# Moving one multiply per tile from VectorE to GpSimd, and column sums behind the next group's matmuls, in an eight-core layer kernel

## The chip, the cores and the metric

The kernel runs on the 8 NeuronCores of one Trainium2 chip, one batch element to a core, with no exchange between cores. The metric is the device time in microseconds of the slowest core. The profile is that of the slowest core (core 1).

## The reference

One layer over x of 8 x 2048 x 2048. A complex diagonal recurrence, a layer norm, a gated feed-forward block with weights rounded to -1, 0, 1 and activations rounded to 8 bits, and a second layer norm. The part that matters here is the second projection:

```python
def _act_quant(a):
    scale = QB / clip(max(abs(a), axis=-1), 1e-05)
    return clip(round(a * scale), -QB, QB) / scale
def _weight_quant(w):
    s = clip(mean(abs(w)), 1e-05)
    return clip(round(w / s), -1.0, 1.0) * s
h = value * silu(gate)                                  # (T, 8192)
h = einsum('bsd,od->bso', _act_quant(h), _weight_quant(w_out))
x = _layernorm(x + (x + h))
```

## The kernel before

Each core works on transposed tensors: features on the partitions, the 2048 time steps along the free dimension. Three stages come before the one of interest: the recurrence, the first layer norm and quantisation, and the gated projection of 64 pairs, which writes h2 (8192 x 2048, bf16) to `h2sp` and the rounded output weights to `wq2sp`. They fill the time up to about 3850 us and are not touched.

The last stage makes the output projection for four blocks q of 512 time steps. `d_mm(q, seg)` does half of the contraction (32 tiles of 128 of h2) for all 2048 outputs, in eight groups dg of two output tiles (ds 0 and 1) each. A group loads its weights in four blocks of 512 KB from the GpSimd queue (L975), into the two halves of `WR`, and runs 16 matmuls on each block (L986). The results of a group go to PSUM banks 0 and 1 of psA, 2 and 3 of psA, or 0 and 1 of psB, in turn. In seg 0 they are copied to `P2` by ScalarE (L1001). In seg 1 there is an epilogue for each of the two tiles: a load of the residual x1 (L1012, on ScalarE's queue), PSUM plus P2 on VectorE (L1018), a product with the scale on GpSimd (L1023), twice x1 added on VectorE (L1028), a store to `z2sp` (L1035), the column sum of the tile by a matmul with ones (L1040), the square on ScalarE (L1048), and the column sum of the squares (L1053). The two sums pile up in banks 3 and 2 of psB.

The moving operand P1 is made by `d_chain(q, seg, j)`, once for each of the 64 tiles of a block: a load of h2 on SyncE's queue (L942) into one of 8 slots of `CBF`, a multiply by the scale (L948) into one of two f32 buffers (`CH_HS` for even j, a part of `MNA` for odd j), and `round_neg`, five steps on VectorE (L246, L248, L250, L253, L256), the last of which writes P1. The 32 chains of (0, 0) are emitted ahead of all groups (`d_quant`); all others are fed between groups: `d_mm` takes a list of functions, and after each group runs the share of it that is due, `take = ceil(rest / groups left)`. While q's seg 0 runs, the chains of its seg 1 are fed, and then the `tail` of the block before: `d_rowsL` (row statistics, two broadcasts through TensorE) and 16 `d_apply_a` (the final norm of one tile each: a load, two GpSimd products L1091 and L1096, a store L1101). While seg 1 runs, the chains of the next block's seg 0 are fed. `d_rowsQ(q + 1)` makes the scale rows of the next block, with two broadcasts that use banks 2 and 3 of psB.

Every engine runs its instructions in the order in which the code emits them. The order is that of the calls; the class `B` adds the waits. It keeps the last writer and the readers of each region, a region being 2 KB of a partition (`GR`), so that two neighbouring 1 KB slots of `CBF` are one region. A wait stands in an engine's queue ahead of the instruction that needs it, and holds all that comes after it.

Of the kernel before, what the change touches and what calls it, by code (L numbers as in the profile page):

```python
# [19 lines left out]
NQ = 4  # L20
# [8 lines left out]
def R(name, e0, e1, es=4):  # L29
    b0, b1 = e0 * es, e1 * es  # L30
    return [(name, i) for i in range(b0 // GR, -(-b1 // GR))]
# [74 lines left out]
def build_program(debug=False):  # L106
    nc = bass.Bass("TRN2", target_bir_lowering=False)
    b = B()
# [828 lines left out]
    def d_chain(q, seg, j):  # L937
        par = q % 2
        jo = seg * 32 + j
        hq = jo % 8  # L940
        hsl = j % 2
        b.dma("sync", lambda s, q=q, jo=jo, hq=hq: s.dma_start(  # L942
            out=CBF[:, hq * 512:(hq + 1) * 512],
            in_=h2sp_t[:, jo, q * 512:(q + 1) * 512]),
            reads=[("h2sp", jo, q // 2)],
            writes=R("CBF", hq * 512, (hq + 1) * 512, es=2))
        src_ap, src_regs = RN[hsl][0], RN[hsl][1]
        b.op("vector", lambda v, hq=hq, src_ap=src_ap, par=par: v.tensor_tensor(  # L948
            src_ap, CBF[:, hq * 512:(hq + 1) * 512], S2B[par],
            OP.mult),  # L950
            reads=R("CBF", hq * 512, (hq + 1) * 512, es=2) +
                  S2R[par],
            writes=src_regs)
        round_neg(hsl,
                  P1[:, seg * 16384 + j * 512:seg * 16384 + (j + 1) * 512],
                  R("P1", seg * 16384 + j * 512,
                    seg * 16384 + (j + 1) * 512, es=2))
# [5 lines left out]
    def d_mm(q, seg, feeder=()):  # L963
        feeder = list(feeder)
        fi = 0
        par = q % 2
        for dg in range(8):
            d0 = dg * 2
            rot = dg % 3
            PSm = [lambda k: PSA(k), lambda k: PSA(2 + k), lambda k: PSB(k)][rot]  # L970
            RRm = [lambda k: RA(k), lambda k: RA(2 + k), lambda k: RB(k)][rot]
            for blk in range(4):
                gj = seg * 32 + blk * 8
                sl = blk % 2
                b.dma("gpsimd", lambda g, dg=dg, gj=gj, sl=sl: g.dma_start(  # L975
                    out=WR[:, sl * 2048:(sl + 1) * 2048].rearrange(
                        "p (j c) -> p j c", j=8),
                    in_=wq2sp[dg, gj // 8]),
                    reads=[("wq2sp", j) for j in range(gj, gj + 8)],
                    writes=R("WR", sl * 2048, (sl + 1) * 2048, es=2),  # L980
                    q="Dwq")
                for jj in range(8):
                    jl = blk * 8 + jj
                    for ds in range(2):
                        b.op("tensor", lambda t, jl=jl, jj=jj, ds=ds, sl=sl,
                             seg=seg, PSm=PSm: t.matmul(  # L986
                            PSm(ds),
                            WR[:, sl * 2048 + jj * 256 + ds * 128:
                               sl * 2048 + jj * 256 + (ds + 1) * 128],
                            P1[:, seg * 16384 + jl * 512:  # L990
                               seg * 16384 + (jl + 1) * 512],
                            start=(jl == 0), stop=(jl == 31)),
                            reads=R("WR", sl * 2048, (sl + 1) * 2048, es=2) +
                                  R("P1", seg * 16384 + jl * 512,
                                    seg * 16384 + (jl + 1) * 512, es=2),
                            writes=[RRm(ds)] if jl in (0, 31) else [],
                            inc=((jj == 7 and ds == 1) or jl == 31))
            if seg == 0:
                for ds in range(2):
                    t_ = dg * 2 + ds  # L1000
                    b.op("scalar", lambda s, ds=ds, t_=t_, PSm=PSm: s.copy(  # L1001
                        P2[:, t_ * 512:(t_ + 1) * 512], PSm(ds)),
                        reads=[RRm(ds)], writes=R("P2", t_ * 512, (t_ + 1) * 512))
                take = -(-(len(feeder) - fi) // (8 - dg))
                for _ in range(take):
                    feeder[fi]()
                    fi += 1
                continue
            for ds in range(2):
                a = d0 + ds  # L1010
                t_ = dg * 2 + ds
                b.dma("scalar", lambda s, q=q, a=a, ds=ds: s.dma_start(  # L1012
                    out=X1S[:, ds * 512:(ds + 1) * 512],
                    in_=x1sp_t[:, a:a + 1, q * 512:(q + 1) * 512]),
                    reads=[("x1sp", a, q)],
                    writes=R("CBF2", ds * 1024, (ds + 1) * 1024, es=2),
                    q="Dscalar")
                b.op("vector", lambda v, ds=ds, t_=t_, PSm=PSm: v.tensor_tensor(  # L1018
                    Z2S[:, ds * 512:(ds + 1) * 512], PSm(ds),
                    P2[:, t_ * 512:(t_ + 1) * 512], OP.add),  # L1020
                    reads=[RRm(ds)] + R("P2", t_ * 512, (t_ + 1) * 512),
                    writes=R("Z2S", ds * 512, (ds + 1) * 512))
                b.op("gpsimd", lambda g, ds=ds, par=par: g.tensor_tensor(  # L1023
                    Z2S[:, ds * 512:(ds + 1) * 512],
                    Z2S[:, ds * 512:(ds + 1) * 512], DQB[par], OP.mult),
                    reads=R("Z2S", ds * 512, (ds + 1) * 512) + DQR[par],
                    writes=R("Z2S", ds * 512, (ds + 1) * 512))
                b.op("vector", lambda v, ds=ds: v.scalar_tensor_tensor(  # L1028
                    Z2S[:, (2 + ds) * 512:(3 + ds) * 512],
                    X1S[:, ds * 512:(ds + 1) * 512], 2.0,  # L1030
                    Z2S[:, ds * 512:(ds + 1) * 512], OP.mult, OP.add),
                    reads=R("CBF2", ds * 1024, (ds + 1) * 1024, es=2) +
                          R("Z2S", ds * 512, (ds + 1) * 512),
                    writes=R("Z2S", (2 + ds) * 512, (3 + ds) * 512))
                b.dma("scalar", lambda s, q=q, a=a, ds=ds: s.dma_start(  # L1035
                    out=z2sp_t[:, a:a + 1, q * 512:(q + 1) * 512],
                    in_=Z2S.ap().rearrange("p (s t) -> p s t", s=4)[:, 2 + ds, :]),
                    reads=R("Z2S", (2 + ds) * 512, (3 + ds) * 512),
                    writes=[("z2sp", a, q)], q="Dscalar")
                b.op("tensor", lambda t, ds=ds, dg=dg: t.matmul(  # L1040
                    psB[0:1, 1536:2048], c_onesc[:],
                    Z2S[:, (2 + ds) * 512:(3 + ds) * 512],
                    start=(dg == 0 and ds == 0), stop=(dg == 7 and ds == 1)),
                    reads=R("Z2S", (2 + ds) * 512, (3 + ds) * 512) + [("c_onesc", 0)],
                    writes=[RB(3)] if (dg, ds) in ((0, 0), (7, 1)) else [],
                    inc=True)
                sqo = 2048 + ds * 512
                b.op("scalar", lambda s, ds=ds, sqo=sqo: s.activation(  # L1048
                    P3[:, sqo:sqo + 512], Z2S[:, (2 + ds) * 512:(3 + ds) * 512],
                    AF.Square),  # L1050
                    reads=R("Z2S", (2 + ds) * 512, (3 + ds) * 512),
                    writes=R("P3", sqo, sqo + 512))
                b.op("tensor", lambda t, ds=ds, dg=dg, sqo=sqo: t.matmul(  # L1053
                    psB[0:1, 1024:1536], c_onesc[:], P3[:, sqo:sqo + 512],
                    start=(dg == 0 and ds == 0), stop=(dg == 7 and ds == 1)),
                    reads=R("P3", sqo, sqo + 512) + [("c_onesc", 0)],
                    writes=[RB(2)] if (dg, ds) in ((0, 0), (7, 1)) else [],
                    inc=True)
            take = -(-(len(feeder) - fi) // (8 - dg))
            for _ in range(take):  # L1060
                feeder[fi]()
                fi += 1

    def d_rowsL(q):
        b.op("vector", lambda v: v.tensor_scalar(
# [42 lines left out]
    tail = []  # L1108
    for q in range(NQ):
        f0 = [(lambda q=q, j=j: d_chain(q, 1, j)) for j in range(32)] + tail  # L1110
        d_mm(q, 0, f0)
        if debug and q == 0:
            b.dma("sync", lambda s: s.dma_start(out=tapA2[:], in_=P1[:]),
                  reads=R("P1", 0, DT * T, es=2), q="Dout")
        if q + 1 < NQ:
            d_rowsQ(q + 1)
            f1 = [(lambda q=q, j=j: d_chain(q + 1, 0, j)) for j in range(32)]
        else:
            f1 = []
# [89 lines left out]
```

How the kernel before makes its waits and increments, by code:

```python
            def emit(engobj, ename):  # L1136
                for item in b.stream[ename]:
                    if item[0] == "w":
                        engobj.wait_ge(semh[item[1]], item[2])
                    else:
                        instr = item[1](engobj)
                        if item[2] is not None:
                            instr.then_inc(semh[item[2]], item[3])
```

## Time and profile before

| | us |
|---|---|
| median of 2 runs | 5914.73 (5914.22 to 5915.24) |
| profiled execution, its own time | 5934.24 |
| span of its slowest core | 5932.6 |
| spans of the eight cores | 5894.7 to 5932.6 |
| granted TensorE clock of the cores | 0.806 to 0.811 |
| busy over the span: TensorE, VectorE, ScalarE, GpSimd | 58%, 43%, 24%, 11% |

The busy shares are means over stages that differ; the section after the next one holds rows of the last stage. Times in the rows are microseconds, counted from the start of the span. In a timeline row they are the start and the duration, then the engine, the line of the code, the operation, what it writes and reads, and in brackets how long the engine was idle before it and what ended that. DVE is VectorE, ACT ScalarE, POOL GpSimd, PE TensorE.

### The profile page before, as it was taken

The page shows a single profiled execution, that of the slowest core. Times are in us where ns is not written, and L with a number is a line of the kernel's source. Part 1 is how long each engine was busy: PE and PEld are TensorE (multiplying, and loading weights), DVE is VectorE, ACT ScalarE, POOL GpSimd, SP SyncE. Part 2 cuts the span into 40 slices and gives each one's busy share as a digit, 9 for nine tenths or more (in the row PEclk, how much of TensorE's full clock was granted, in tenths as well). Part 3 has the DMA queues.
Part 4 walks back from the last instruction along what each step waited for, and adds up shares of the span by engine and source line. Part 5 has one row for each costly group of instructions (what it writes and reads, how often), then busy time and mean ns, then how long its engine had stood idle before and what let it go on. Part 6 is the DMA issues. An engine that isn't in the chain of part 4 may idle for free.

```text
span 5932.6 us, 43701 instructions; the slowest of 8 cores (5894.7 to 5932.6 us)
## 1 busy us (share of the span) xinstructions
PE 3460.7 (58%) x13489; PEld 1332.3 (22%) x13489; DVE 2559.3 (43%) x3497; ACT 1404.4 (24%) x1134; POOL 645.8 (11%) x805
## 2 busy tenths in 40 slices
PE   1223321404888787777767799737782674476273
PEld 0100000001333333332323244302231221122121
DVE  1331844845333333333333344487673466158101
ACT  2222122132554444433444433200000000000000
POOL 0210000000000000000000000001112211311314
PEclk9866765756999898888888899859896887788686
DMA  8223445364555455565556632114442442343233
GB/s 220 78 92 106 130 155 168 127 213 159 184 192 186 159 140 146 135 136 130 145 131 143 131 101 94 39 57 129 134 147 77 127 138 93 114 129 123 97 114 105
DMA packets 211694, 774.78 MB, mean 131 GB/s; under 512 B 24412, under 2 KB 61439, under 8 KB 161799
## 3 DMA queue, kind: packets, MB, share of 16 engines
q10 hardware_dynamic: 64512, 318.80, 16.4%
q0 software_dynamic: 68832, 243.32, 14.9%
q1 hardware_dynamic: 78120, 209.87, 12.7%
q8 instruction: 110, 1.80, 0.1%
q14 instruction: 120, 0.98, 0.1%
HBM read 662.83 MB, written 117.44 MB: 132 GB/s over the span
## 4 chain that ended last, share of the span: by engine, by line
DMA 35%; PE 21%; DVE 17%; ACT 11%; issue 10%; POOL 5%; DVEq 1%; ACTq 0%; POOLq 0%; SPq 0%
DMA WOF<-woutT 8%; PE psA L986 6%; DMA WOF<-wgvL 5%; DMA WR<-wgvL 5%; DMA wq2sp<-P 4%; PE psA L784 4%; PE psB L784 4%; DMA WR<-wq2sp 3%; ACT HBF L734 3%; DMA WR<-woutT 3%; DMA CBF<-x1sp 2%; ACT P L745 2%; ACT WR L748 2%; DVE HBF L796 2%; ACT CBF L730 2%
## 5 line engine op out<-in xcount | busy, mean ns | idle before, releaser
L986 PE MATMUL psA<-P,WR 128*128 128x512 bf16 x3072 | 730.9, 396 | 414.4 <-DMA WR<-wq2sp 309.7
L784 PE MATMUL psA<-P,CBF 128*128 128x512 bf16 x2048 | 510.6, 410 | 233.5 <-DVE CBF L738 223.9
L784 PE MATMUL psA<-P,MNA 128*128 128x512 bf16 x2048 | 506.6, 407 | 211.6 <-DVE MNA L738 202.1
L986 PEld LDWEIGHTS psA<-P,WR 128*128 128x128 bf16 x3072 | 300.2, 101 | 878.2 <-issue 575.0
L784 PE MATMUL psB<-P,CBF 128*128 128x512 bf16 x2048 | 457.4, 379 | 9.6
L784 PE MATMUL psB<-P,MNA 128*128 128x512 bf16 x2048 | 457.4, 379 | 9.6
L752 DVE TENSOR_TENSOR P<-P,WR 128x2048 bf16<-128x2048 bf16 x64 | 78.4, 1226 | 739.2 <-ACT WR L748 739.2
L784 PEld LDWEIGHTS psA<-P,CBF 128*128 128x128 bf16 x2048 | 210.8, 104 | 532.0 <-issue 341.4
L784 PEld LDWEIGHTS psA<-P,MNA 128*128 128x128 bf16 x2048 | 209.8, 103 | 506.9 <-issue 313.4
L398 ACT ACTIVATE WOF<-WOF 128x2048 f32<-128x2048 f32 x96 | 183.5, 1911 | 402.8 <-DMA WOF<-wgvL 258.3
L745 ACT ACTIVATE P<-WOF,colS 128x2048 bf16<-128x2048 f32 x64 | 128.2, 2003 | 615.8 <-DMA wq2sp<-P 335.5
L1048 ACT ACTIVATE P<-Z2S 128x512 f32<-128x512 f32 x64 | 40.4, 631 | 978.4 <-DVE Z2S L1018 519.6
L398 ACT ACTIVATE WR<-WR 128x2048 f32<-128x2048 f32 x96 | 183.5, 1911 | 359.9 <-DMA WR<-wgvL 247.1
L806 ACT ACTIVATE HBF<-HBF 128x1024 f32<-128x1024 f32 x128 | 135.2, 1056 | 515.1 <-DVE HBF L796 515.1
L784 PEld LDWEIGHTS psB<-P,CBF 128*128 128x128 bf16 x2048 | 197.8, 98 | 264.1 <-issue 39.3
L784 PEld LDWEIGHTS psB<-P,MNA 128*128 128x128 bf16 x2048 | 197.7, 98 | 264.2 <-issue 39.3
L734 ACT ACTIVATE HBF<-P,colS 128x2048 bf16<-128x2048 f32 x128 | 254.4, 1988 | 0.0
L809 DVE TENSOR_TENSOR CBF<-CBF,HBF 128x1024 bf16<-128x1024 f32 x128 | 156.9, 1225 | 223.8 <-ACT HBF L806 223.8
L975 POOL DMA_DIRECT2D WR<-wq2sp x256 | 137.4, 537 | 1045.6 <-PE psA L986 780.5
L986 PE MATMUL psB<-P,WR 128*128 128x512 bf16 x1024 | 232.6, 384 | 30.3 <-DMA WR<-wq2sp 30.3
L834 POOL DMA_DIRECT2D h2sp<-CBF x128 | 70.4, 550 | 1545.3 <-DVE CBF L809 1369.8
L225 PE MATMUL psA<-REP,c_ones 1*128 1x512 f32 x16 | 15.4, 1059 | 348.6 <-DVE REP L582 204.2
(217 smaller groups left out, 4169.3 us busy)
## 6 DMA issues: line engine op xcount, KB each, us to landing
P<-wgvL SPq DMA_DIRECT2D x128, 1024.0 KB
WR<-wq2sp POOLq DMA_DIRECT2D x256, 512.0 KB, 3.9
WOF<-woutT ACTq DMA_DIRECT2D x96, 1024.0 KB, 6.6
WOF<-wgvL ACTq DMA_DIRECT2D x64, 1024.0 KB, 5.0
WR<-wgvL ACTq DMA_DIRECT2D x64, 1024.0 KB, 5.0
h2sp<-CBF POOLq DMA_DIRECT2D x128, 256.0 KB, 4.5
WR<-woutT ACTq DMA_DIRECT2D x32, 1024.0 KB, 5.1
wq2sp<-P POOLq DMA_DIRECT2D x64, 512.0 KB, 8.4
```

Source lines behind the costliest of these rows:

```text
L398: b.op("scalar", lambda s, slot=slot, buf=buf: s.activation(buf, buf, AF.Abs, accum_out=slots[:, slot:slot + 1]), reads=breg, writes=breg ...
L730: b.op("scalar", lambda s, sl=sl: s.activation(WQap(sl), WV[:, sl * 2048:(sl + 1) * 2048], AF.Sign, bias=colS[:, 1:2]), reads=R("P2", sl * ...
L734: b.op("scalar", lambda s, sl=sl, SGa=SGa: s.activation(SGa, WV[:, sl * 2048:(sl + 1) * 2048], AF.Sign, bias=colS[:, 0:1]), reads=R("P2", ...
L745: b.op("scalar", lambda s: s.activation(WOQ[:, 0:2048], WOF[:], AF.Sign, bias=colS2[:, 1:2]), reads=R("WOF", 0, 2048) + [("colS2", 0)], wr ...
L748: b.op("scalar", lambda s: s.activation(WR[:, 2048:4096], WOF[:], AF.Sign, bias=colS2[:, 0:1]), reads=R("WOF", 0, 2048) + [("colS2", 0)], ...
L752: b.op("vector", lambda v: v.tensor_tensor(WOQ[:, 0:2048], WOQ[:, 0:2048], WR[:, 2048:4096], OP.add), reads=R("P3", 2048, 3072) + R("WR", ...
L784: sv=sv, last=last: t.matmul(PS[:, (vg * 2 + tq) * 512:(vg * 2 + tq + 1) * 512], WQap(sv + vg)[:, a * 128:(a + 1) * 128], P1[:, a * T + th ...
L796: b.op("vector", lambda v, PS=PS, th=th: v.tensor_tensor(GS[:, 0:1024], PS[:, 1024:2048], dqa1rep[:, th * 1024:(th + 1) * 1024], OP.mult), ...
L806: b.op("scalar", lambda s: s.activation(SIL[:, 0:1024], GS[:, 0:1024], AF.Silu), reads=R("HBF2", 0, 2048, es=2), writes=R("HBF2", 2048, 40 ...
L809: b.op("vector", lambda v, hsl=hsl: v.tensor_tensor(H2T[:, hsl * 1024:(hsl + 1) * 1024], T2[:, 0:1024], SIL[:, 0:1024], OP.mult), reads=R( ...
L975: b.dma("gpsimd", lambda g, dg=dg, gj=gj, sl=sl: g.dma_start(out=WR[:, sl * 2048:(sl + 1) * 2048].rearrange("p (j c) -> p j c", j=8), in_= ...
L986: seg=seg, PSm=PSm: t.matmul(PSm(ds), WR[:, sl * 2048 + jj * 256 + ds * 128: sl * 2048 + jj * 256 + (ds + 1) * 128], P1[:, seg * 16384 + j ...
```

## The change

Three things are edited. The multiply of each chain goes from VectorE to GpSimd. In seg 1 the two column sums of each tile are kept back and emitted after the next group's matmuls (those of the last group after its feeder). And `d_rowsQ(q + 1)` becomes the last item of the feeder of `d_mm(q, 0)` rather than a call after it, which makes that list one longer.

```diff
-        b.op("vector", lambda v, hq=hq, src_ap=src_ap, par=par: v.tensor_tensor(
+        b.op("gpsimd", lambda g, hq=hq, src_ap=src_ap, par=par: g.tensor_tensor(
             src_ap, CBF[:, hq * 512:(hq + 1) * 512], S2B[par],
             OP.mult),
...
+        late = []
         for dg in range(8):
...
+            for f in late:
+                f()
+            late = []
             if seg == 0:
...
-                b.op("tensor", lambda t, ds=ds, dg=dg: t.matmul(
-                    psB[0:1, 1536:2048], c_onesc[:],
...
+                def mk_sum(ds=ds, dg=dg):
+                    b.op("tensor", lambda t, ds=ds, dg=dg: t.matmul(
+                        psB[0:1, 1536:2048], c_onesc[:],
+                        Z2S[:, (2 + ds) * 512:(3 + ds) * 512],
...
+                late.append(mk_sum)
...
+                def mk_sumsq(ds=ds, dg=dg, sqo=sqo):
+                    b.op("tensor", lambda t, ds=ds, dg=dg, sqo=sqo: t.matmul(
+                        psB[0:1, 1024:1536], c_onesc[:], P3[:, sqo:sqo + 512],
...
+                late.append(mk_sumsq)
             take = -(-(len(feeder) - fi) // (8 - dg))
             for _ in range(take):
                 feeder[fi]()
                 fi += 1
+        for f in late:
+            f()
...
         f0 = [(lambda q=q, j=j: d_chain(q, 1, j)) for j in range(32)] + tail
+        if q + 1 < NQ:
+            f0.append(lambda q=q: d_rowsQ(q + 1))
         d_mm(q, 0, f0)
...
         if q + 1 < NQ:
-            d_rowsQ(q + 1)
             f1 = [(lambda q=q, j=j: d_chain(q + 1, 0, j)) for j in range(32)]
```

## Rows read from the trace of the kernel before

**Rows 1.** Window: length, then PE, PEld, DVE, ACT, POOL busy; clock, DMA share, GB/s
```profile
4344.00:4495.00 151.00, 92.12 (x392) 36.91 (x390) 127.89 (x217) 7.40 (x14) 13.75 (x25) 0.84 0.38 120
```

**Rows 2.** Waits from 3840 us to the end: total, times, longest
```profile
POOL WR L975 <- PE psA L986: 780.5, 119, 45.4
...
PE psB L1040 <- DVE Z2S L1028: 198.9, 64, 6.5
...
DVE Z2S L1028 <- DMA CBF<-x1sp: 156.2, 32, 7.4
```

**Rows 3.** Timeline, VectorE: one chain and the start of the next
```profile
4192.41 0.68 DVE L948 TENSOR_TENSOR CH_HS<-CBF,MXA 128x512 f32<-128x512 bf16 x1
...
4193.20 0.43 DVE L246 CAST CH_I<-CH_HS 128x512 int32<-128x512 f32 x1
...
4196.46 0.69 DVE L948 TENSOR_TENSOR MNA<-CBF,MXA 128x512 f32<-128x512 bf16 x1
```

**Rows 4.** Timeline: epilogue of a group in seg 1 and the next group's start
```profile
4231.40 0.69 DVE L1018 TENSOR_TENSOR Z2S<-psA,P 128x512 f32<-128x512 f32 x1 [2.49 <-PE psA L986]
...
4235.17 1.26 POOL L1023 TENSOR_TENSOR Z2S<-Z2S,REP 128x512 f32<-128x512 f32 x1 [1.68 <-DVE Z2S L1018]
...
4239.99 0.69 DVE L948 TENSOR_TENSOR CH_HS<-CBF,MXA 128x512 f32<-128x512 bf16 x1
...
4243.73 6.50 PE L986 MATMUL psA<-P,WR 128*128 128x512 bf16 x29
...
4244.92 0.69 DVE L948 TENSOR_TENSOR MNA<-CBF,MXA 128x512 f32<-128x512 bf16 x1 [0.79 <-DMA CBF<-h2sp]
```

**Rows 5.** Timeline: VectorE and GpSimd at once; then L931, min/median/max ns
```profile
242.04 2.28 DVE L471 TENSOR_TENSOR P<-P,MXA 128x2048 f32<-128x2048 f32 x1
...
242.39 6.28 POOL L473 TENSOR_TENSOR P<-P,MNA 128x2048 f32<-128x2048 f32 x1 [25.14 <-DVE P L463]
...
5009.43 1.54 POOL L1096 TENSOR_TENSOR OTS<-Z2S,MXA 128x512 f32<-128x512 f32 x1 [0.20 <-POOL Z2S L1091]
...
5009.95 1.29 DVE L931 TENSOR_SCALAR MXA<-MXA,srow 1x512 f32<-1x512 f32 x1
...
L931 DVE TENSOR_SCALAR MXA<-MXA,srow x2: 474/884/1293, 4122.1 to 5010.0; 1x512 f32<-1x512 f32 x2
```

**Rows 6.** Timeline: weight loads and first matmuls; first and last of eight L1018
```profile
4521.07 1.14 POOL L975 DMA_DIRECT2D WR<-wq2sp  x2
...
4525.53 9.57 PE L986 MATMUL psA<-P,WR 128*128 128x512 bf16 x32 [20.00 <-DMA WR<-wq2sp]
...
4535.64 0.53 POOL L975 DMA_DIRECT2D WR<-wq2sp  x1 [2.92 <-PE psA L986]
...
4623.04 8.61 PE L986 MATMUL psA<-P,WR 128*128 128x512 bf16 x32 [29.82 <-DMA WR<-wq2sp]
...
4640.23 0.69 DVE L1018 TENSOR_TENSOR Z2S<-psA,P 128x512 f32<-128x512 f32 x1 [46.14 <-PE psA L986]
...
4837.86 0.69 DVE L1018 TENSOR_TENSOR Z2S<-psA,P 128x512 f32<-128x512 f32 x1 [2.01 <-PE psA L986]
```

**Rows 7.** First chains (min/median/max ns, first and last start); timeline: landmarks, two output tiles
```profile
L948 DVE TENSOR_TENSOR CH_HS<-CBF,REP x64: 683/685/687, 3855.0 to 4987.0; 128x512 f32<-128x512 bf16 x64
...
4117.78 3.33 DVE L922 RECIPROCAL MXA<-P 1x512 f32<-1x512 f32 x1
...
4125.46 9.93 PE L986 MATMUL psA<-P,WR 128*128 128x512 bf16 x32
...
4513.28 1.27 POOL L1091 TENSOR_TENSOR Z2S<-Z2S,MXA 128x512 f32<-128x512 f32 x1
...
4517.18 1.27 POOL L1091 TENSOR_TENSOR Z2S<-Z2S,MXA 128x512 f32<-128x512 f32 x1
...
4574.40 9.03 PE L986 MATMUL psA<-P,WR 128*128 128x512 bf16 x32 [31.53 <-DMA WR<-wq2sp]
...
5123.69 0.59 PE L986 MATMUL psA<-P,WR 128*128 128x512 bf16 x1 [29.48 <-DMA WR<-wq2sp]
```

More of the change, by code:

```diff
@@ L1039, in d_mm @@
                     writes=[("z2sp", a, q)], q="Dscalar")
-                b.op("tensor", lambda t, ds=ds, dg=dg: t.matmul(
-                    psB[0:1, 1536:2048], c_onesc[:],
[L1042 to L1046, printed above, removed]
+                def mk_sum(ds=ds, dg=dg):
+                    b.op("tensor", lambda t, ds=ds, dg=dg: t.matmul(
+                        psB[0:1, 1536:2048], c_onesc[:],
+                        Z2S[:, (2 + ds) * 512:(3 + ds) * 512],
+                        start=(dg == 0 and ds == 0), stop=(dg == 7 and ds == 1)),
+                        reads=R("Z2S", (2 + ds) * 512, (3 + ds) * 512) +
+                              [("c_onesc", 0)],
+                        writes=[RB(3)] if (dg, ds) in ((0, 0), (7, 1)) else [],
+                        inc=True)
+                late.append(mk_sum)
                 sqo = 2048 + ds * 512
@@ L1052, in d_mm @@
                     writes=R("P3", sqo, sqo + 512))
[L1053 to L1058, printed above, removed]
+                def mk_sumsq(ds=ds, dg=dg, sqo=sqo):
+                    b.op("tensor", lambda t, ds=ds, dg=dg, sqo=sqo: t.matmul(
+                        psB[0:1, 1024:1536], c_onesc[:], P3[:, sqo:sqo + 512],
+                        start=(dg == 0 and ds == 0), stop=(dg == 7 and ds == 1)),
+                        reads=R("P3", sqo, sqo + 512) + [("c_onesc", 0)],
+                        writes=[RB(2)] if (dg, ds) in ((0, 0), (7, 1)) else [],
+                        inc=True)
+                late.append(mk_sumsq)
             take = -(-(len(feeder) - fi) // (8 - dg))
```

## The prediction

> **Terms.** Stage D makes the output projection for four column blocks q. In each there are two passes, seg 0 and seg 1, of eight groups dg; a group is 64 matmuls fed by four weight loads (L975), numbered WR0 to WR3 here. A "chain" is one quantised tile of h2: one multiply (L948) and five rounding steps (L246 to L256), all on VectorE before.
>
> **What bounds the kernel now.** The change touches only stage D, which begins near 3850 us, so I read the windows first. While the chains of a second pass are made, VectorE is busy 127.9 of 151 us and TensorE 92 [rows 1]: that stretch is VectorE's. The waits come next, for seg 1: TensorE stands 198.9 us for the tile that its column sum reads, and VectorE 156.2 us for the residual tile x1 from memory. The largest wait of all is GpSimd's, 780.5 us in 119 pieces, for TensorE to free a weight buffer [rows 2]. It costs nothing by itself, but it tells where GpSimd stands: in its queue at a weight load, behind TensorE. Whatever is queued after that load stands too. That is what the change has to be read against, because the multiply moves to this queue.
>
> **What one chain costs.** In the timeline a chain starts at 4192.41, its first rounding step at 4193.20, the next chain at 4196.46: 4.05 us, of which 0.79 is the multiply and 3.26 the rest [rows 3]. If VectorE were alone the change would give back 0.79 x 256 = 202 us of its time.
>
> **What a multiply costs on GpSimd.** No multiply of bf16 by f32 stands there before; the nearest row, f32 by f32 of the same 128x512, is 1.26 us [rows 4]. I take 1.26. A shorter one would help little, since the waits below are longer.
>
> **Both engines at once.** At 242.04 VectorE starts a 2.28 us product of two SBUF tiles, at 242.39 GpSimd starts one that lasts 6.28 us, though four times the size of a 1.26 us one would be below 5.1: the difference is about the 1.93 us that VectorE still had to run. The other way round, VectorE's one-row L931, 0.47 us alone, takes 1.29 us when started at 5009.95 beside a GpSimd product that ends at 10.97 [rows 5]. So they shut each other out rather than share. Each chain of five steps will meet one multiply, and so pays 0.82 more: 3.26 + 0.82 = 4.08, and a little for a second step that is touched. I take p = 4.2 us a chain. Bounds: 3.3 (no meeting) and 4.7 (all 1.26 us lost and a restart of 0.2). The saving of 0.79 is thus eaten before queues are looked at.
>
> **The queue.** GpSimd runs in order: WR0 to WR3 of a group, then (seg 1) its two products L1023, then the group's multiplies, then WR0 of the next group. There are only two source buffers, so multiply k+2 waits until chain k has ended. Hence WR0 of the next group waits for the chains, and the multiplies wait for WR3, which waits for TensorE's second block. TensorE and VectorE, which overlapped, take turns. Also, two neighbouring slots of h2 share a dependency region, so the load of an odd tile is issued only when the even multiply before it is over, and lands in at most 3.36 us without a wait or 4.24 with one [rows 3, 4]; I take 3.75. n multiplies then take about (n-1)p: 12.6 us for 4, 16.8 for 5, 21.0 for 6, 25.2 for 7, 130.2 for the 32 at the start.
>
> Three more durations. Weight load to first matmul: 4521.07 to 4525.53, w = 4.5. First matmul to the end of WR3's issue: 10.6 from 4525.53 after 20 us of idle, at 0.22 us a matmul (29 in 6.50, [rows 4]) only 7.7; after the 10 to 20 us of idle expected I take c = 9.7. First matmul to L1018: 4623.04 to 4640.23, s = 17.2 [rows 6].
>
> **A. The start and seg 0 of q = 0.** Before: first chain 3855.0, first matmul of seg 1 at 4125.46, 270.5 us [rows 7]; weights were loaded early and the first group ran beside the chains. After: 130.2 + 4.5 = 134.7 to the first matmul. The feeder grows from 32 to 33 items (d_rowsQ), so the groups take 5, 4, ... 4 of them. Group 0: 9.7 + 16.8 + 4.5 = 31.0. Six groups: 9.7 + 12.6 + 4.5 = 26.8 each, 160.8. The last: 9.7 + 12.6 + 5.7 for the chains still running = 28.0, and d_rowsQ with its broadcasts 7.7 as before (4117.78 to 4125.46). Sum 362.2: **+92**.
>
> **B. Seg 1 of q = 0, 1, 2**, 7 steps from group to group each. Before: 4640.23 to 4837.86 is 7 steps of 28.2 [rows 6]. After, from L1018 of the first tile (4231.40 in [rows 4]): the second L1023 ends at +5.0, multiply 0 at 6.3, the odd load at 10.0, multiply 1 at 11.7 (with 0.4 of shutting out). Chain 0 starts at 8.6 to 9.2, as L1028 waits for x1 as ever, and ends at 13.4; multiply 2 at 15.0; load at 18.7; multiply 3 at 20.4; WR0 and w: 24.9. Then s: 42.1. +13.9 x 21 = **+292**. The column sums put behind the next group's matmuls (four of about 1 us) fall in TensorE's idle time, and buy nothing here: WR0 comes later than they did.
>
> **C. From the last L1018 of a seg 1 through the next seg 0**, three times. Before: 4837.86 to 5123.69, 285.8 [rows 6, 7]. After: 24.9; with 50 items (7, 7, 6, 6, 6) two groups of 9.7 + 25.2 + 4.5 = 39.4 and three of 35.2; the fifth group with d_rowsL: 17.2, 3 for the broadcasts (estimate), 5 output tiles at 3.9 (4513.28 to 4517.18), 4.5: 44.2; then one group as before, 4574.40 to 4623.04 = 48.6, and one with a tile less, 44.7 [rows 7]. Sum 346.7: +61 x 3 = **+183**. For q = 3 the feeder has 49 items, with one tile moved and the same sum.
>
> **D. Seg 1 of q = 3** has no feeder. WR0 can go when L1023 ends at 4236.43, and TensorE starts at 4240.9 in place of 4243.73 [rows 4]: 2.8 x 7 = **-20**. This is all that the late sums bring. d_rowsQ moved into the feeder's last place is emitted where it stood: nothing.
>
> **Sum**: 92 + 292 + 183 - 20 = +547. On the span of 5932.6 that is 6480, with the 1.6 us around it 6481. The median of the runs is 19.5 below the profiled execution, so 6461, say **6460 us**.
>
> **Bounds.** p stands in the sum about 57 times in A, 21 in B, 81 in C. p = 3.3 gives 143 us less, 4.7 gives 80 more. With c at 7.7 and s two less: 88 less; c at 10.6: 21 more. The likeliest case alone: 6360 to 6570.
>
> **Rivals.**
> 1. The engines don't meet (other than [rows 5] says; the multiply fits into the gaps of 0.1 us or the bf16 input changes it): p = 3.3, 6318. The queue alone still gives +400. 15%.
> 2. Every multiply costs its whole length and GpSimd is also held off by the next step: p = 4.7, 6540. L931's 0.82 speaks against the first half; nothing in the trace tells who gets in first. 20%. The Trainium skill's rule above ("SBUF — State Buffer") speaks for it.
> 3. Faster. GpSimd reaches the multiplies ahead of VectorE, so a chain is 3.26 and TensorE is freed of the sums: 0.79 x (64 + 3 x 36) = 136, and 2.8 x 28 = 78, so 5915 - 214 = 5701. It decides if a group's multiplies start before WR3 has waited; the order written in the code and the 780.5 us of waiting [rows 2] speak against it. 4%.
> 4. The turns are shorter, for instance because the multiplies are over before TensorE's idle matters: a coupling of a third of mine, 6100. The 4.5 us of w in every step speaks against it. 6%.
> My case: 55%.
>
> Within 2% (about what a measurement of this kernel can tell from no change) lies only the edge of 3 and 4: 3%; faster 4%; slower 93%. The range 6280 to 6590 takes in 1 and 2.
>
> **What would show it.** After: L975's wait on TensorE becomes small, and it waits for multiplies; L948 on GpSimd waits for L256. Between groups of seg 1 TensorE idles some 20 us, not 12; first matmuls about 42 apart. In seg 0 with 4 chains groups are 27 apart, not 16. Casts L246, L248 or steps beside a multiply show 1.2 us and more instead of 0.43 or 0.69. TensorE's granted clock falls in stage D. I am wrong if chains run at 3.3, if L975 still waits for TensorE 780 us, or if the multiplies start before the second block of their group ends.

## The result: 7.6% slower

| | before | changed |
|---|---|---|
| median of the runs, us | 5952.02 (10 runs, 5914.22 to 6040.58) | 6389.47 (11 runs, 6372.54 to 6490.38) |
| span of the profiled core | 5932.6 | 6374.0 |
| stage D: first multiply (L948) to the end of the span | 2077.6 | 2532.3 |

The ratio is 1.0759, 95% interval 1.0717 to 1.08. Some executions of either kernel run with a lower granted clock on one die or both and take longer; the medians in the table are of all executions, and every ratio here compares only the faster ones of both kernels. The forecast was 6460 us, 1.092 of the 5914.73 known then. The stage D line is taken from the first start of L948 (3855.0 in [rows 7], 3841.71 below) to the end of the span. The time ahead of that stage differs by up to 100 us from one profiled execution to the next (3788 to 3889 us in the traces used here) though no edit touches it, so where two kernels are close I compare this stage. In it the eight cores of one execution still differ by 10 to 24 us (2065.7 to 2080.5 before, 2522.9 to 2536.0 changed; 53 us in e8), so smaller differences of the slowest core say nothing.

The page of the changed kernel, the span in 40 slices (each digit of PE is tenths of busy time, of PEclk tenths of the full clock):

```profile
PE   1224232108887777777778981655534554454464
PEclk9757666559998988888889995877767777777787
```

From the 26th slice on TensorE is busy 30% to 60% of the time, and its granted clock is mostly 0.7 of full. No engine is full there (the digits of VectorE and GpSimd on the same page are at most 6 and 3): the work goes round in turns.

Waits of the changed kernel after 3840 us (total, times, longest), to be read beside [rows 2]:

```profile
PE psA L987 <- DMA WR<-wq2sp: 849.8, 103, 32.4
POOL WR L976 <- PE psA L987: 593.1, 96, 19.0
...
PE psB L987 <- DMA WR<-wq2sp: 262.4, 35, 21.5
...
POOL CH_HS L948 <- DVE P L256: 188.7, 71, 3.9
...
POOL MNA L948 <- DMA CBF<-h2sp: 154.0, 54, 4.2
POOL MNA L948 <- DVE P L256: 148.4, 48, 4.0
```

TensorE waits for weights (L976 is L975 of before, L987 is L986) for 849.8 + 262.4 = 1112 us; before, the waits view of the same stretch had 310 and 30. GpSimd, which issues them, waits 337 us for the rounding step L256 to free a source buffer. These are the links of the forecast: weights behind multiplies, multiplies behind rounding.

One step of seg 1 in the changed kernel, timeline from L1022 (L1018 of before) on; compare [rows 4]:

```profile
4282.94 0.69 DVE L1022 TENSOR_TENSOR Z2S<-psB,P 128x512 f32<-128x512 f32 x1 [16.72 <-PE psB L987]
...
4286.78 1.26 POOL L1027 TENSOR_TENSOR Z2S<-Z2S,REP 128x512 f32<-128x512 f32 x1 [1.75 <-DVE Z2S L1022]
...
4288.00 1.16 POOL L948 TENSOR_TENSOR CH_HS<-CBF,MXA 128x512 f32<-128x512 bf16 x1
4290.36 0.69 DVE L1032 SCALAR_TENSOR_TENSOR Z2S<-CBF,Z2S 128x512 f32<-128x512 f32 x1 [3.72 <-DMA CBF<-x1sp]
...
4291.61 1.32 POOL L948 TENSOR_TENSOR MNA<-CBF,MXA 128x512 f32<-128x512 bf16 x1 [2.45 <-DMA CBF<-h2sp]
...
4295.21 1.21 POOL L948 TENSOR_TENSOR CH_HS<-CBF,MXA 128x512 f32<-128x512 bf16 x1 [2.28 <-DVE P L256]
...
4299.23 1.21 POOL L948 TENSOR_TENSOR MNA<-CBF,MXA 128x512 f32<-128x512 bf16 x1 [2.82 <-DVE P L256]
...
4300.39 1.12 POOL L976 DMA_DIRECT2D WR<-wq2sp  x2
...
4304.15 8.85 PE L987 MATMUL psA<-P,WR 128*128 128x512 bf16 x32 [17.58 <-DMA WR<-wq2sp]
...
4320.77 0.69 DVE L1022 TENSOR_TENSOR Z2S<-psA,P 128x512 f32<-128x512 f32 x1 [14.40 <-PE psA L987]
```

The four multiplies (L948) stand one after another, the weight loads directly behind the last, and TensorE is idle for 17.6 us. Before, the loads went at 4236.38, 5 us after L1018; here they go 17.5 us after.

The chain itself, VectorE and GpSimd at the start of the stage in the changed kernel; compare [rows 3] and [rows 5]:

```profile
3841.71 1.15 POOL L948 TENSOR_TENSOR CH_HS<-CBF,REP 128x512 f32<-128x512 bf16 x1 [9.59 <-DVE REP L229]
...
3855.32 0.42 DVE L246 CAST MNA<-MNA 128x512 int32<-128x512 f32 x1
3855.54 1.21 POOL L948 TENSOR_TENSOR CH_HS<-CBF,REP 128x512 f32<-128x512 bf16 x1 [2.82 <-DVE P L256]
3855.84 1.19 DVE L248 CAST MNA<-MNA 128x512 f32<-128x512 int32 x1
3857.14 0.69 DVE L250 TENSOR_TENSOR MNA<-MNA 128x512 f32<-128x512 f32 x1
...
3859.34 0.42 DVE L246 CAST CH_I<-CH_HS 128x512 int32<-128x512 f32 x1
3859.57 1.21 POOL L948 TENSOR_TENSOR MNA<-CBF,REP 128x512 f32<-128x512 bf16 x1 [2.81 <-DVE P L256]
3859.86 1.20 DVE L248 CAST CH_CF<-CH_I 128x512 f32<-128x512 int32 x1
```

A chain takes 4.02 us (3855.32 to 3859.34), where it took 4.05 with the multiply on VectorE. The cast L248, 0.43 us alone, is not over until the multiply of the next tile is: it takes 1.19 to 1.20 us. So moving the multiply off VectorE gave back 0.03 us a chain.

### The profile page after: what moved, and what is told of

The parts are those of the page before. It is cut to its first block, busy times and chain, and to the rows that moved or that the text cites. A ratio compares the mean times of both kernels' runs of the same rounds, so it can differ in the third digit from the quotient of the medians.

```text
span 6374.0 us, 44356 instructions; the slowest of 8 cores (6347.8 to 6374.0 us)
## 1 busy us (share of the span) xinstructions
PE 3458.8 (54%) x13489; PEld 1358.0 (21%) x13489; DVE 2539.2 (40%) x3241; ACT 1403.0 (22%) x1134; POOL 952.2 (15%) x1061
## 3 DMA queue, kind: packets, MB, share of 16 engines
q14 instruction: 125, 1.02, 0.1%
## 4 chain that ended last, share of the span: by engine, by line
DMA 34%; PE 23%; DVE 16%; ACT 10%; issue 10%; POOL 5%; DVEq 0%; ACTq 0%; POOLq 0%; SPq 0%
PE psA L987 9%; DMA WOF<-woutT 7%; DMA WR<-wq2sp 6%; DMA WOF<-wgvL 5%; DMA WR<-wgvL 5%; DMA wq2sp<-P 4%; PE psA L784 4%; PE psB L784 4%; PE psB L987 3%; ACT HBF L734 3%; DMA WR<-woutT 2%; ACT P L745 2%; ACT WR L748 2%; DVE HBF L796 2%; ACT CBF L730 1%
## 5 line engine op out<-in xcount | busy, mean ns | idle before, releaser
L987 PE MATMUL psA<-P,WR 128*128 128x512 bf16 x3072 | 779.4, 417 | 978.2 <-DMA WR<-wq2sp 849.8
L987 PEld LDWEIGHTS psA<-P,WR 128*128 128x128 bf16 x3072 | 316.6, 105 | 1456.8 <-issue 1180.9
L987 PE MATMUL psB<-P,WR 128*128 128x512 bf16 x1024 | 264.7, 423 | 262.5 <-DMA WR<-wq2sp 262.4
L976 POOL DMA_DIRECT2D WR<-wq2sp x256 | 138.6, 542 | 795.3 <-PE psA L987 593.1
L1022 DVE TENSOR_TENSOR Z2S<-psA,P 128x512 f32<-128x512 f32 x48 | 33.0, 688 | 550.6 <-PE psA L987 550.6
```

Of the source, the lines that this page charges most:

```text
L976: b.dma("gpsimd", lambda g, dg=dg, gj=gj, sl=sl: g.dma_start(out=WR[:, sl * 2048:(sl + 1) * 2048].rearrange("p (j c) -> p j c", j=8), in_= ...
L987: seg=seg, PSm=PSm: t.matmul(PSm(ds), WR[:, sl * 2048 + jj * 256 + ds * 128: sl * 2048 + jj * 256 + (ds + 1) * 128], P1[:, seg * 16384 + j ...
```

## The experiments

My theory: the loss is the order of GpSimd's queue, in which the next group's weights stand behind the multiplies, with the chain at about its old length because the two engines shut each other out. Rivals: the sums kept back cost TensorE its clock; the odd loads of h2 are late; the multiply on GpSimd, or the shutting out, is the loss by itself.

All ratios are to the kernel before on the same chip; e1 to e4 ran on one chip, e5 to e8 on a second, e9 and e10 on a third. The last column is stage D of the slowest core of one profiled execution.

| run | ratio (95% interval) | stage D, us |
|---|---|---|
| before | 1 | 2077.6 |
| changed kernel | 1.0759 (1.0717 to 1.08) | 2532.3 |
| e1 multiply only | 1.0752 (1.0696 to 1.0809) | 2527.7 |
| e2 sums only | 0.9991 (0.9954 to 1.0028) | 2076.5 |
| e3 changed, h2 slots 2 KB apart | 1.0772 (1.0696 to 1.0849) | 2531.7 |
| e4 e3 with weights on SyncE's queue | 0.9346 (0.9287 to 0.9404) | 1710.0 |
| e5 before, slots and weights as e4 | 0.9551 (0.9447 to 0.9654) | 1831.4 |
| e6 e5 with the sums kept back | 0.9411 (0.9345 to 0.9477) | 1743.2 |
| e7 e5 with an idle GpSimd product per chain | 0.9835 (0.9728 to 0.9941) | 1986.5 |
| e8 changed, weights on SyncE's queue, old slots | 1.0243 (1.013 to 1.0356) | 2172.1 |
| e9 e4 with x1 loaded ahead | 0.9324 (0.9298 to 0.935) | 1677.7 |
| e10 e9 with the multiply on VectorE | 0.932 (0.9295 to 0.9346) | 1669.3 |

### Which part of the change costs: e1 and e2

e1 is the kernel before with the first line of the diff alone:

```diff
-        b.op("vector", lambda v, hq=hq, src_ap=src_ap, par=par: v.tensor_tensor(
+        b.op("gpsimd", lambda g, hq=hq, src_ap=src_ap, par=par: g.tensor_tensor(
```

> The multiply moved to GpSimd, nothing else. Queue theory (weight loads stand behind the group's multiplies in GpSimd's queue): nearly the whole loss is here, ratio to the kernel before 1.07 to 1.085, steps from group to group in seg 1 about 38.5 us as in the changed kernel, because the column sums fit into the time in which TensorE waits for its weights anyway. Rival (the sums put behind the next group's matmuls leave TensorE idle and its clock low, and that is a large part of the loss): 1.03 to 1.05.

e2 is the change without that line.

> Only the column sums are kept back (and d_rowsQ is a feeder item); the multiply stays on VectorE. My account: TensorE's next group starts some 3 us earlier but after 6 us of real idle its first block runs at the lower clock, 6.9 us in place of 4.2, as in the last seg 1 of the changed kernel (steps 27.7 against 28.4). So -0.7 x 28 = -20 us, ratio 0.995 to 1.0. Rival (the 198.9 us of waiting for the sums are really given back): ratio 0.97 to 0.985.

Measured: 1.0752 and 0.9991. The multiply is the whole loss; in e1 the steps of seg 1 are 39.0 us (L1018 at 4155.02, 4194.49, 4233.29, 4272.51, 4311.17), with the sums where they always were, so the rival that the sums kept back make the loss by TensorE's clock is out. The sums alone are worth little or nothing: the interval of e2 holds both 1 and my 0.9966. Its stage is 1.1 us shorter on the slowest core and 10 us on the median of the eight cores (2064.5 for 2074.4), with cores that differ by 24 us among themselves, so a few us of gain are not ruled out. The rival that the 198.9 us of waiting in [rows 2] are given back is out. In its place TensorE's wait for weights grew from 309.7 to 458.3 us on psA and from 30.3 to 81.0 on psB. In e2 the sums run at once behind a group, and the next group still waits for its weights, now with nothing to do meanwhile:

```profile
4115.04 1.02 PE L1062 MATMUL psB<-P,c_onesc 128*1 128x512 f32 x2
4123.58 8.56 PE L987 MATMUL psB<-P,WR 128*128 128x512 bf16 x32 [7.52 <-DMA WR<-wq2sp]
```

### The odd load of h2: e3

```diff
-        hq = jo % 8
+        hq = 2 * (jo % 4)
```

> The changed kernel with h2 slots 2 KB apart (four in place of eight), so that the load of an odd tile no longer waits for the even multiply. Its wait in GpSimd's queue (154 us for the odd multiplies) goes, but VectorE's 4.02 us a chain bounds most of it: some 0.8 us less in each of 21 steps of seg 1, 2.5 us in each of 13 groups of seg 0 that start on an even tile, -50 us in all: ratio to the kernel before about 1.067 where the changed kernel has 1.076. If the odd loads were a main cause of the loss: below 1.05.

Measured: 1.0772, stage 0.6 us shorter on the slowest core. The 50 us did not come. The wait of the odd multiply for its load is gone from the trace, yet another wait came in its place: the multiplies stand 497.6 us for L256 in place of 337. In seg 1 the weights did go sooner, 17.1 us after L1022 for 18.2 (means of 21 steps; 4238.06 to 4254.85 in this one), but most of that was lost before TensorE had started: from the issue of the weights to the first matmul it was 4.5 us for 3.8, and the first 32 matmuls took 9.2 for 9.0:

```profile
4254.85 1.12 POOL L976 DMA_DIRECT2D WR<-wq2sp  x2
...
4259.42 9.91 PE L987 MATMUL psA<-P,WR 128*128 128x512 bf16 x32 [17.73 <-DMA WR<-wq2sp]
```

So the odd load is not a cause of the loss. Why the weights took longer from issue to use is open.

### The queue: e4 and e8

e4 is e3 with the weight loads on another queue:

```diff
-                b.dma("gpsimd", lambda g, dg=dg, gj=gj, sl=sl: g.dma_start(
+                b.dma("sync", lambda g, dg=dg, gj=gj, sl=sl: g.dma_start(
                     out=WR[:, sl * 2048:(sl + 1) * 2048].rearrange(
...
```

> As the run before with slots 2 KB apart, and the weight loads moved from GpSimd's queue to SyncE's. The multiply stays on GpSimd. Queue theory: TensorE no longer waits for multiplies; chains stay at 4.0 us. Seg 1 steps 25.5 us (VectorE: epilogue 9.3 and four chains of 4.0), in the last block about 16, and the output tiles no longer hold the weights (3 x 65 us): about 5915 - 350, ratio 0.93 to 0.96. Rival (the loss is the two engines shutting each other out, or the multiply's own latency in the chain): ratio stays above 1.04.

e8 has this edit without the slots: in SyncE's queue the load of an odd tile then waits for the even multiply, and the next group's weights stand behind it.

> The changed kernel with only the weight loads moved to SyncE's queue; the eight h2 slots of 1 KB stay, so that a load of an odd tile in that queue waits for the even multiply, and the next group's weights stand behind it. If it is the order in a queue that costs, and not which queue, part of the loss returns: the weights go about 4 us sooner than in the changed kernel, in 21 steps of seg 1 and some 26 groups of seg 0, the output tiles no longer hold them: ratio 0.98 to 1.02. If leaving GpSimd's queue were enough: 0.935.

Measured: 0.9346 and 1.0243. The multiply stayed on GpSimd and met VectorE as before in both. Steps of seg 1 in e4 (timeline, VectorE):

```profile
4139.86 0.68 DVE L1022 TENSOR_TENSOR Z2S<-psB,P 128x512 f32<-128x512 f32 x1
...
4164.38 0.68 DVE L1022 TENSOR_TENSOR Z2S<-psA,P 128x512 f32<-128x512 f32 x1
```

24.5 us, and no wait for TensorE ahead of either: what sets the pace is VectorE's own order of work, with its waits for the product and for x1 inside it.

In e8 the old pattern is back with another engine's queue:

```profile
4252.26 1.21 POOL L948 TENSOR_TENSOR CH_HS<-CBF,MXA 128x512 f32<-128x512 bf16 x1 [3.34 <-DVE P L256]
...
4254.02 0.84 SPq L976 DMA_DIRECT2D WR<-wq2sp  x2
...
4257.89 4.42 PE L987 MATMUL psB<-P,WR 128*128 128x512 bf16 x10 [15.20 <-DMA WR<-wq2sp]
```

The weights go when the third multiply has ended (4252.26 + 1.21) and the load that waited for it has been issued. The steps are 37.6 us (4201.18 to 4314.08, three), where I had expected 35 and a ratio of 0.98 to 1.02. Part of the excess is the clock of these executions: the profiled one had 0.755 to 0.764 over the span on all eight cores, the other kernels on that chip 0.81 to 0.83, and each of the other three of e8 had a die at 0.77 to 0.78. The slowest core of each of the three dies of e8 that had 0.81 took 5913 to 5933 us, that of the ten such dies of the kernel before on that chip 5838 to 5869: some 1.01 (an estimate from these spans), within the forecast. The 2172.1 us of the table carry the lower clock too.

So it is what a queue makes the weights wait for, and not the engine that the multiply runs on. e8 tells that from "leaving GpSimd's queue is enough", and also from "SyncE's queue moves the weights faster": a weight load took 3.7 us from issue to landing in the changed kernel (median), 4.3 in e4 and 3.8 in e8.

### Is the multiply worth moving where no weights stand behind it: e5, e6, e10

e5 is the kernel before with the two edits of e4 (slots, SyncE's queue).

> The kernel before, only with the weight loads on SyncE's queue and h2 slots 2 KB apart. If the gain of the run with both edits is that of the queue, it is here too without the multiply's move: chains 4.05 us in place of 4.02. But the column sums now hold TensorE after each group of seg 1, which matters where no chains fill the time: in the last block about 25 us a group, not 16, 70 us more. Ratio 0.94 to 0.96. If moving the multiply to GpSimd is worth something once the queue is free: above 0.97.

e6 is e4 with the multiply back on VectorE.

> As e5 and with the column sums kept back; that is, the whole change but the multiply's move, with weight loads on SyncE's queue. Expected like the run with the multiply on GpSimd: 0.93 to 0.94, since a chain costs 4.05 us here and 4.02 there. If the sums kept back are worth nothing as in the kernel before: as e5. If GpSimd's multiply relieves VectorE: 0.95 or more.

Measured: 0.9551 and 0.9411. e6, which has the multiply on VectorE, has nearly the whole gain of e4. Once the weights no longer wait, the sums kept back are worth 88 us of stage D (1831.4 to 1743.2), in the last block above all (60 of them): after the first, its steps are 18.4 to 19.6 us with the sums kept back and 25.6 to 27.3 without.

The move itself is another matter. e4 is 33 us of stage D shorter than e6, more than the cores of one execution differ (1696.5 to 1710.0 against 1725.4 to 1744.5), and its steps in the first three blocks are 1.1 us shorter on the mean of all cores (24.7 for 25.7). The traces show where that can come from. In e4 GpSimd makes two multiplies while VectorE stands idle for x1:

```profile
4144.93 1.16 POOL L948 TENSOR_TENSOR CH_HS<-CBF,MXA 128x512 f32<-128x512 bf16 x1
4146.04 1.16 POOL L948 TENSOR_TENSOR MNA<-CBF,MXA 128x512 f32<-128x512 bf16 x1
...
4149.21 0.69 DVE L1032 SCALAR_TENSOR_TENSOR Z2S<-CBF,Z2S 128x512 f32<-128x512 f32 x1 [5.65 <-DMA CBF<-x1sp]
```

From there to the next group's L1022 VectorE needs 15.2 us (4149.21 to 4164.38), in e6 with its own multiplies 16.8 (4135.91 to 4152.73). But the two ran on different chips, and their ratios (0.9346 and 0.9411) overlap, so this gain of some 30 us is likely and not shown. Where x1 comes early it is gone: e10, below, is level with e9 on one chip.

### The price of the two engines at once: e7

To e5 a product on a scratch buffer is added that nobody reads, one for each chain:

```diff
+        b.op("gpsimd", lambda g, par=par: g.tensor_tensor(
+            GS[:, 0:512], GS[:, 512:1024], S2B[par], OP.mult),
+            reads=R("HBF2", 1024, 2048, es=2) + S2R[par],
+            writes=R("HBF2", 0, 1024, es=2))
```

> e5 with one more product on GpSimd for every chain, of the same size, on a scratch buffer that no one reads: nothing depends on it and no weight load stands behind it. If the two engines shut each other out, each costs VectorE's chain 0.8 us: chains 4.85 us, up to 200 us over e5, ratio 0.97 to 0.985. If they share: the same as e5. A wrong reading of the lock (the whole 1.2 us each): 0.99 to 1.0.

Measured: 0.9835, stage D 155 us longer than e5's. Groups of e7 in stage D (busy, mean ns):

```profile
L954 POOL TENSOR_TENSOR HBF<-HBF,REP 128x512 f32<-128x512 f32 x128 | 181.7, 1419 | 27.0 <-DVE REP L229 9.6 <-POOL HBF L954 0.4
...
L253 DVE SCALAR_TENSOR_TENSOR CH_CF<-CH_HS,CH_CF 128x512 f32<-128x512 f32 x128 | 100.8, 788 | 14.0 <-DVE CH_HS L250 0.9
...
L246 DVE CAST CH_I<-CH_HS 128x512 int32<-128x512 f32 x128 | 76.5, 598 | 13.3
...
L948 DVE TENSOR_TENSOR CH_HS<-CBF,MXA 128x512 f32<-128x512 bf16 x64 | 65.1, 1018 | 0.0
```

Every step of the chain grew against e5: L253 788 ns for 692, L246 598 for 427, L948 1018 for 685. The products grew too, 1419 ns for the 1260 of [rows 4]. No chain waits for such a product and no product for a chain, so what is left is that the engines meet. 155 us for 256 products is 0.6 us each, within the 200 us that 0.8 each allows; the rest may be products that fall where VectorE waits anyway. By the Trainium skill, "SBUF — State Buffer", section "Who interferes with whom", a VectorE step with two SBUF inputs or a cast in a two-port mode and a GpSimd step that reads SBUF exclude each other for a whole instruction. This trace agrees that both kinds grow: the cast L246 from 427 to 598 ns on the mean, L253 with its two inputs from 692 to 788.

### The version that beats both: e9 and e10

In e9 the two x1 loads of a group go ahead of its epilogue in ScalarE's queue, since in e4 VectorE waited 123 us there:

```diff
             for ds in range(2):
                 a = d0 + ds
-                t_ = dg * 2 + ds
                 b.dma("scalar", lambda s, q=q, a=a, ds=ds: s.dma_start(
                     out=X1S[:, ds * 512:(ds + 1) * 512],
...
+            for ds in range(2):
+                a = d0 + ds
+                t_ = dg * 2 + ds
```

> The faster version (multiply on GpSimd, sums kept back, weights on SyncE's queue, slots 2 KB apart) with both x1 loads of a group emitted ahead of its epilogue, so that the second no longer stands behind the first tile's square in ScalarE's queue. VectorE, which now sets the pace of seg 1 with 24.5 us a group, waited about 4 us there for x1 (123 us in all). Expected -3 to -4 us in each of 21 to 28 groups: 5503 less 60 to 110 us, ratio 0.915 to 0.925. If something else is late next (weights on their queue, PSUM banks): 0.93 to 0.935.

> The same with the multiply back on VectorE: the change's first part alone, tested where no weight load stands behind it. Chains 4.05 us in place of 4.02 with 256 of them, so 8 us slower at most: ratio within 0.005 of the run before. If the multiply on GpSimd relieves VectorE once x1 is early: over 0.01 slower than the run before.

Measured: 0.9324 and 0.932. Steps of seg 1 in e9, VectorE:

```profile
4161.74 0.68 DVE L1024 TENSOR_TENSOR Z2S<-psA,P 128x512 f32<-128x512 f32 x1
...
4183.95 0.68 DVE L1024 TENSOR_TENSOR Z2S<-psB,P 128x512 f32<-128x512 f32 x1
```

22.2 us in place of 24.5: 2.3 less, not 3 to 4, because L1034 and the first cast now meet the multiplies:

```profile
4167.15 1.35 DVE L1034 SCALAR_TENSOR_TENSOR Z2S<-CBF,Z2S 128x512 f32<-128x512 f32 x1 [1.72 <-POOL Z2S L1029]
4167.92 1.61 POOL L948 TENSOR_TENSOR MNA<-CBF,MXA 128x512 f32<-128x512 bf16 x1
4168.43 1.38 DVE L246 CAST CH_I<-CH_HS 128x512 int32<-128x512 f32 x1
```

Stage D is 32 us shorter than e4's (on another chip), but the ratio moved by 0.002, inside its interval: the expected 0.915 to 0.925 was too good. The steps of the last block, which has no chains, did not gain but grew, from 18.6 to 19.6 us on the mean of all cores; why is open. e10 with the multiply on VectorE is the same within both intervals, and its stage D, 8 us shorter, lies within what the cores of one execution differ. So with weights on a queue that nothing slow stands in and the sums kept back, the multiply may stay where it was: 0.941 of the kernel before (e6), and 0.932 with x1 ahead (e10).

## Why the prediction was right

The direction, the place and the mechanism held; the size was 547 us forecast and 455 measured in stage D. Three of the four terms came out 108 us smaller together than forecast; the fourth, a gain, brought 15 of its 20 us less, and by luck that offset a part. Term by term, landmarks as in the forecast:

| term | forecast | measured |
|---|---|---|
| p, one chain | 4.2 | 4.02 |
| multiply, bf16 by f32 | 1.26 | 1.16 to 1.21 |
| group of seg 0 with 4 chains | 26.8 | 25.0 to 26.9, mean 25.8 (six, first matmuls 4000.68 to 4155.72) |
| A, start to seg 1 of q = 0 | 362.2, +92 | 345.1, +75 |
| B, 21 steps of seg 1 | 42.1 each, +292 | 38.8 each, +216 |
| C, last L1018 through the next seg 0, three times | 346.7 each, +183 | 345.6, 339.4, 337.5, +168 |
| D, last seg 1 | -20 | -5 (steps of 27.7 for 28.4) |

- **The queue.** Right, shown by e4 and e8.
- **The engines shut each other out, so the saving of 0.79 us a chain is eaten.** Right, in both traces and by e7. A multiply costs VectorE 0.77 us (L248 1.20 for 0.43), the forecast took 0.82. The rival that they do not meet (p = 3.3) is out; so is p = 4.7. The multiply itself is hardly held off: its row begins 0.22 us into L246 and lasts 1.21 us, for 1.15 in the stage's first one. One reading of [rows 5] in the forecast does not add up, though nothing hangs on it: 6.28 less four times 1.26 is 1.24 us, not the 1.93 that VectorE still had to run.
- **B, the term most off.** 292 forecast, 216 measured. The step that was mis-sized is the time of the last multiply: it ends 20.4 us after L1018 in the forecast, and the weights go 18.2 us after L1022 in the traces (mean of the 21 steps, 17.5 in the one above). I had let each odd multiply wait 3.75 us for its load. The first waited 2.45, and the second not at all beyond the chain: it starts 4.02 us after multiply 2 started, when VectorE has ended a chain, and 2.8 us after that multiply ended, so its load took no longer than that. The rest is w, 3.8 us and not 4.5, and s, 16.9 and not 17.2.
- **D.** The start was right, the gain wrong. The weights are issued 5.0 us after L1018 in the kernel before and 5.0 after L1022 in the changed one, and the first matmul goes earlier, 9.5 us after L1022 for 12.7, because TensorE is no longer held by the sums. But then the first 32 matmuls take 9.7 us for 7.3 (means of seven groups), and nearly all is lost again. What failed is the sentence that takes all of an earlier start for gain. The 5 us are no gain to count on either: over all eight cores the steps are 28.05 us before and 28.01 in the changed kernel. In the kernel before the sums ran on TensorE while it waited, and the first block after them ran at full clock. Kept back, they are done at once, TensorE is idle for 6 us, and its first block runs at the lower clock. Windows of the last seg 1 (length, PE busy with count, PEld, DVE, ACT, POOL, granted clock, DMA share, GB/s): from the first matmul of a group, in the kernel before and in e1; then the changed kernel's idle stretch, the first 7 us of its group and the 3.5 us behind them:

```profile
5800.79:5808.40 7.61, 7.08 (x33) 3.05 (x32) 0.00 (x0) 0.00 (x0) 0.53 (x1) 1.00 0.25 80
```

```profile
6134.77:6141.77 7.00, 7.00 (x33) 3.05 (x32) 0.00 (x0) 0.00 (x0) 0.53 (x1) 1.00 0.27 87
```

```profile
6176.80:6182.70 5.90, 0.00 (x0) 0.00 (x0) 0.82 (x2) 0.63 (x1) 2.32 (x3) 0.92 0.77 247
6182.74:6189.70 6.96, 6.96 (x20) 2.52 (x21) 0.00 (x0) 0.61 (x1) 0.00 (x0) 0.58 0.29 90
6189.70:6193.20 3.50, 2.95 (x14) 1.16 (x12) 0.00 (x0) 0.00 (x0) 0.54 (x2) 1.00 0.42 150
```

  Granted 1.00 against 0.58: 33 matmuls in 7.1 us there, 20 in 7.0 here. 0.58 of full clock is a stretch mostly at 1.2 GHz of the two levels, 1.2 and 2.4. e1 against the changed kernel tests this, since only the sums (and the place of `d_rowsQ`) differ: in the seven groups of the last seg 1 the granted clock over the first 7 us is 1.00 in e1 and 0.61 in the changed kernel, the first 32 matmuls take 7.1 and 9.7 us, and the steps are 27.68 and 27.71. e2, on the chip of e1 and with the sums kept back, has 0.62 and 9.7 us. So the sums in the gap kept the clock up, and keeping them back gains an earlier start and loses it to the clock.
- **A marker that failed.** "L975's wait on TensorE becomes small": it fell from 780.5 to 593.1 us only (956.5 to 774.4 with psB). Nearly all of it, 126 waits in 64 groups, is now the third and fourth block inside a group, which still wait for TensorE. The markers that held: L948 waits for L256 (337 us), casts of 1.2 us, 17.6 us of idle TensorE, groups 25 to 27 us apart in seg 0 and 38.8 in seg 1, and a granted clock of 0.787 over the span for 0.806.
- **C.** Near in sum, by parts that offset: the groups of seg 0 with chains were mostly shorter, and the one with d_rowsL took 50.4 us (first matmuls 4674.98 and 4725.41) where I had 44.2.
- **The median.** 6389 against 6460 lies in the range, on the side of a smaller p and a smaller B.

## What to carry to other kernels

Before an operation is moved to a less busy engine, list what its queue already issues for others, transfers above all: the operation's own waits become theirs. Here one multiply per tile made the weight loads of the next group wait for VectorE's rounding, and moving 256 multiplies cost 455 us in place of the 202 us that they took on VectorE and that the move was meant to save. With the loads on a queue without such a wait, and h2 slots that do not bring one in, the same multiply costs nothing, and the kernel is 6.5% faster than before (e4). Most of that gain comes without the move (e6). And between VectorE and GpSimd, count a moved operation on both engines if they read SBUF at the same time.

## What the runs showed of the hardware

- The two engines take turns instruction by instruction. A product of bf16 by f32, 128x512, takes 1.15 us on GpSimd at the start of stage D (3841.71), where VectorE has nothing but a copy out of PSUM; a cast of 0.43 us on VectorE that meets one takes 1.20, and GpSimd's own product grows to 1.61 when it meets two steps (e9).
- A product of bf16 by f32 on GpSimd took 1.15 to 1.21 us where little met it, little less than f32 by f32 with 1.26.
- An earlier start of TensorE after an idle stretch can be lost whole to the clock. With the sums kept back the first matmul of a group came 2.7 us earlier than in e1 (9.5 us after the epilogue's first step for 12.2), and the first 32 matmuls took 2.6 us longer (9.7 for 7.1).
- A weight load of 512 KB took about as long from issue to landing from either queue (medians: 3.9 us before, 3.7 changed, 4.1 e3 from GpSimd's; 4.3 e4, 3.9 e5, 3.8 e8, 4.6 e9 from SyncE's); what it waited for ahead of its issue made the difference between 1.076 and 0.935.
